# Tensor places in SBUF: weights of the last layer and of the down product in tensors of their own, attention, state and key tensors moved by 64-byte blocks

## The chip, the cores and the metric

The kernel runs on one core of one Trainium2 chip. The metric is the device time of one execution in microseconds (us), the median over several runs. The core has five engines that run side by side and wait for each other through semaphores: TensorE (PE; its weight loads are listed apart as PEld), VectorE (DVE), ScalarE (ACT), GpSimd (POOL) and SyncE (SP), which issues the transfers.

## What is computed

The input x has 16 sequences of 512 tokens with 256 features. Two branches start from the same layer norm, and both are added to x:

```python
xn = _layernorm(x, axis=-1)
x = x + attn(xn) + ffn(xn)
# attn: x @ up_w.T, a causal convolution of width 4, silu; q, k, g, tau projections;
#       gated linear attention in chunks, state 64 x 512; times silu(gate); rms norm; @ down_w.T
# ffn
h = jax.nn.silu(_tlin(x, w1_w, w1_s)) * _tlin(x, w2_w, w2_s)
h = jax.nn.gelu(_tlin(h, h1_w, h1_s), approximate=False)
h = jax.nn.gelu(_tlin(h, h2_w, h2_s), approximate=False)
return _tlin(h, w3_w, w3_s)
```

The ffn weights are ternary (-1, 0, 1), of sizes 256 to 1024 (w1, w2), 1024 to 1024 (h1, h2) and 1024 to 256 (w3).

## The kernel before, in words

**Tiling.** A sequence is worked off in two halves of 256 tokens, so there are 32 halves. A loop of 15 rounds (`rounds`) runs both halves of a sequence, and the last sequence stands behind it. All weights lie in SBUF from the start on. They come in 27 chunks of 128 x 1024 elements; each goes by DMA into a staging slot, from there ACT copies it into its place as fp32r, and DVE makes the low part (for `up`, `gate`, `proj`, `down`) or compares it with the original (for the ternary ones). Each activation is kept as a high and a low fp32r tensor, so that a product with ternary weights takes two matmuls, and one with the other weights three.

**Order of a half on TensorE.** z and up products, layer 1 (w1, w2) mixed with gate and input gate, transposes, the q/k/g/tau projection, layer h1, the small products of the attention, layer h2, in its middle `state_update` (first half of a sequence only, L604 to L607) and `outputs` (L613 to L628), transposes of the next layer norm (L453), layer w3 (32 matmuls of 256 columns), the down product (24 matmuls of 256 columns), and the sum for the rms norm (L679, two products, recorded as four). All of the wide products are issued by the helper `wide`, so they have one line, L383. The order is written out by hand in the program. There is no scheduler.

**Who is stationary and who moves.** `pe.matmul(out, a, b)` loads `a` into the array and streams `b` through it; a profile row prints `out<-b,a`: what moves comes first. In the hidden layers the weights (`wwhole`) are stationary and the activations (`xnth`, `xntl`, `hid0h`, `hid0l`, `hid1h`, `hid1l`) move. In w3 and in the down product it is the other way round: the activations are stationary (`hid0h`, `hid0l`; `parth`, `partl`) and the weights move (`wwhole`; `whi`, `wlo`). In `outputs`, `parth` and `partl` (then `vh`, `vl`, the values) are stationary and `atth`, `attl` move; in the second half of a sequence `stateh` and `statel` are stationary too, and `kdq` (then the queries) moves. In `state_update`, `kdq` (then the keys) is stationary and `parth`, `partl` move.

```python
for c in range(NC):                                                # w3, L383 through wide
    mm = wide(fb[2 * c][:, 0:H], [(a, wb) for a in parts(exact, hid0h[:, k, t], hid0l[:, k, t])], ...)
pairs += [(parth[:, k, t], wh), (partl[:, k, t], wh), (parth[:, k, t], wl)]   # down
first = [(vh[:, 0, cols], atth[:]), (vh[:, 0, cols], attl[:]), (vl[:, 0, cols], atth[:])]   # outputs
```

**Places.** Tensors are laid end to end in a partition, each start rounded up to 32 bytes. `lie_off(n)` puts in a gap so that the next tensor starts n blocks of 64 bytes behind the place of `wwhole`, modulo 512 bytes. In what follows a **place** is that number, 0 to 7 (`wwhole` is at 0 by definition). A step within a tensor (another weight block, another k) is a multiple of 512 bytes in all of the products named here, so that the place of an operand is that of its tensor.

**Probes that are in the program.** While the weights still come in, TensorE runs filler products without use for the result: `plain(bank, count, weights_at, moving_at)` issues `count` matmuls of 256 columns, stationary from `whi` shifted by `weights_at` elements of 4 bytes, moving from `wwhole` shifted by `moving_at` elements. 16 elements are one block of 64 bytes. `shifted` issues, for each pair in its list, two narrow products and then 14 of the full size. The lists, in the order of the program (L424 and L428):

```python
plain(3, 34)
shifted(0, [(0, 16), (0, 32)])
shifted(2, [(0, 48), (0, 64), (0, 80), (0, 96)])
shifted(2, [(0, 112), (0, 128), (0, 8), (8, 8), (16, 0), (32, 0), (64, 0), (80, 160), (24, 104), (16, 96)])
```

Of the kernel before, what the change touches and what calls it, by code (L numbers as in the profile page):

```python
# [6 lines left out]
F32 = mybir.dt.float32  # L7
F32R = mybir.dt.float32r
ALU = mybir.AluOpType
ACT = mybir.ActivationFunctionType  # L10

P = 128
# [25 lines left out]
COMB = CHUNKS.index("comb")  # L38
SPLIT = {"up": 0, "gate": 1, "proj": 2, "down": 3}


LOADS = [(n, m) for n in ("w1", "h1", "h2") for m in range(FB)] + [("w3", 0), ("w3", 1)]

WHOLE = {n: i for i, n in enumerate(c for c in CHUNKS if c not in SPLIT and c != "comb")}

# [34 lines left out]
def layer_program(nc, x, stage_w, ig1t, ig2t, convw, convb, projb, resw, normw, s1, s2, sh1, sh2, s3, ident,  # L80
                  masks, out):
    ctx = ExitStack()
    with ctx:
        def sb(name, shape, dt=F32):
            return ctx.enter_context(nc.sbuf_tensor(name, shape, dt))
# [23 lines left out]
        wwhole_place = next_place()  # L109
        wwhole = sb("wwhole", [P, len(WHOLE), STAGE], F32R)  # L110
        whi = sb("whi", [P, len(SPLIT), STAGE], F32R)
# [26 lines left out]

        xin = sb("xin", [P, HALVES, NC, H])
        lie_off(7)  # L140
        xnth, xntl = sb("xnth", [P, HB, N], F32R), sb("xntl", [P, HB, N], F32R)
# [32 lines left out]
        sqsum = work[:, DB * N + NC * H:]  # L174
        att = sb("att", [P, NC, CH])
        atth, attl = sb("atth", [P, 2, CH], F32R), sb("attl", [P, 2, CH], F32R)
        stateh, statel = sb("stateh", [P, DI], F32R), sb("statel", [P, DI], F32R)
        kdq = sb("kdq", [P, N], F32R)
        kd, qhl = kdq[:].rearrange("p (c a k) -> p c a k", c=NC, a=2), kdq[:]
# [73 lines left out]
        def stage_slot(n):  # L253

            return (sgate[:].rearrange("p d t -> p (d t)"), shift[:].rearrange("p d t -> p (d t)"),
                    v[:].rearrange("p c d -> p (c d)"), raw[:].rearrange("p a b t -> p (a b t)"), stage_more[:, 0, :], stage_more[:, 1, :],
                    mixed[:], small[:, 0:STAGE])[n % SLOTS]

        def rows(c):
# [119 lines left out]
        def _(pe):  # L379
# [14 lines left out]
            def ffn_weight(exact, name, k, m):  # L394


                if exact:
                    return (wwhole[:, WHOLE[f"w3{k // 4}"], (k % 4) * H:(k % 4 + 1) * H] if name == "w3" else
                            wwhole[:, WHOLE[f"{name}{k}"], m * P:(m + 1) * P])
                if name == "w3":  # L400
                    return stream[:, LOADS.index((name, k // 4)) % 2, (k % 4) * H:(k % 4 + 1) * H]
                if name == "w2":
                    name, k = "w1", HB + k
                return stream[:, LOADS.index((name, m)) % 2, k * P:(k + 1) * P]
# [13 lines left out]

            up, w10 = whi[:, SPLIT["up"], :], wwhole[:, WHOLE["w10"], :]

# [39 lines left out]
            def half(seq, p, last, exact):  # L460
# [207 lines left out]
                for c in range(NC):  # L668
                    t = slice(c * CH, (c + 1) * CH)
                    pairs = []  # L670
                    for k in range(DB):
                        wh, wl = split_w("down", k, 0, H, H)
                        pairs += [(parth[:, k, t], wh), (partl[:, k, t], wh), (parth[:, k, t], wl)]
                    mm = wide(ab[3][:, c * H:(c + 1) * H], pairs)
# [27 lines left out]
        def _(act):  # L702
# [7 lines left out]
            for n, name in enumerate(CHUNKS):  # L710
# [8 lines left out]
                if name == "down":  # L719
                    for d in range(DB):  # L720
                        mul = act.activation(whi[:, SPLIT[name], d * H:(d + 1) * H], stage_slot(n)[:, d * H:(d + 1) * H], ACT.Copy,
                                             scale=normw_s[:, d:d + 1])
                    mul.then_inc(prep_act, 1)
                elif name in SPLIT:
                    act.activation(whi[:, SPLIT[name], :], stage_slot(n), ACT.Copy).then_inc(prep_act, 1)
                else:
                    act.activation(wwhole[:, WHOLE[name], :], stage_slot(n), ACT.Copy).then_inc(prep_act, 1)  # L727

# [160 lines left out]
        def _(dve):  # L889
# [42 lines left out]
            for n, name in enumerate(CHUNKS):  # L932
# [30 lines left out]
                dve.wait_ge(prep_act, n + 1)  # L963
                if name in SPLIT:
                    if name == "down":
                        for d in range(DB):
                            t = slice(d * H, (d + 1) * H)
                            st = dve.scalar_tensor_tensor(wlo[:, SPLIT[name], t], stage_slot(n)[:, t], normw_s[:, d:d + 1],
                                                          whi[:, SPLIT[name], t].bitcast(F32), ALU.mult, ALU.subtract)
                        st.then_inc(prep_dve, 1)  # L970
                    else:
                        low(wlo[:, SPLIT[name], :], stage_slot(n), whi[:, SPLIT[name], :]).then_inc(prep_dve, 1)
                else:

                    if n > 1:
                        dve.wait_ge(prep_dve, n - 1)
                    dve.scalar_tensor_tensor(flags[:, n % 2, :], stage_slot(n), 1.0, wwhole[:, WHOLE[name], :].bitcast(F32), ALU.mult,
                                             ALU.not_equal, accum_out=inexact[:, WHOLE[name]:WHOLE[name] + 1]).then_inc(prep_dve, 1)
# [347 lines left out]
```

## Time and profile before

| what | value |
|---|---|
| median of 3 runs | 1945.26 us (1943.17 to 1946.41) |
| the profiled execution | 1944.75 us |
| span of its instructions | 1943.0 us |
| PE busy | 1926.5 us (99%) |
| PEld, weight loads | 1907.6 us (98%) |
| DVE / ACT / POOL busy | 1586.9 (82%) / 1296.4 (67%) / 81.2 us (4%) |
| granted TensorE clock | 0.998 |
| PE's share of the chain that ended last | 95% |

A matmul's record lasts longer than the time that it takes from its successor: they overlap. A 256-column matmul has a record of 276 to 283 ns, while the next one starts some 113 to 120 ns later. What counts for the time is this distance from start to start, called the **interval** below. Where a timeline row has n equal matmuls in one stretch without a gap, its second number is n - 1 intervals and one record.

### The profile page before, as it was taken

How to read it: one execution, taken by the hardware profiler on the slowest of the kernel's cores; microseconds unless marked ns; L12 is line 12 of the kernel's file. 1: busy time of each engine (PE TensorE's matmuls, PEld its weight loads, DVE VectorE, ACT ScalarE, POOL GpSimd, SP SyncE). 2: the span in 40 equal slices, each digit the busy share in tenths (PEclk: the TensorE clock that was granted, in tenths of full speed). 3: DMA queues.
4: the chain of work that ended last, by engine and by line, in shares of the span. 5: the costliest groups of instructions: out<-in, count | busy, mean ns of one | idle time of the engine just before them, and what ended most of it. 6: DMA issues, size and time to landing. Idle time of an engine off the chain costs nothing.

```text
span 1943.0 us, 46120 instructions
## 1 busy us (share of the span) xinstructions
PE 1926.5 (99%) x16804; PEld 1907.6 (98%) x16804; DVE 1586.9 (82%) x4304; ACT 1296.4 (67%) x2687; POOL 81.2 (4%) x136
## 2 busy tenths in 40 slices
PE   8999999999999999999999999999999999999998
PEld 7999999999999999999999999999999999999998
DVE  7788888888788887888888788787888878878887
ACT  5676667766676766666766677675667666667565
POOL 0000000000000000000000000000000000000000
PEclk9999999999999999999999999999999999999999
DMA  8000000000000000000000000000000000000000
GB/s 308 7 12 12 12 2 12 12 12 12 12 1 12 12 12 12 11 2 12 12 12 12 7 7 12 12 12 12 1 12 12 12 12 12 1 12 12 13 7 8
DMA packets 23538, 34.19 MB, mean 18 GB/s; under 512 B 3170, under 2 KB 19810, under 8 KB 23364
## 3 DMA queue, kind: packets, MB, share of 16 engines
q1 hardware_dynamic: 23364, 31.43, 4.8%
q8 instruction: 162, 2.65, 0.6%
q14 instruction: 12, 0.10, 0.0%
HBM read 23.04 MB, written 8.39 MB: 16 GB/s over the span
## 4 chain that ended last, share of the span: by engine, by line
PE 95%; issue 2%; ACT 1%; DVE 1%; SPq 1%; DMA 0%; POOLq 0%; POOL 0%; DVEq 0%; ACTq 0%
PE fb L383 65%; PE ab L383 21%; PE ab L593 2%; PE ab L628 1%; PE ab L529 1%; PE ab L518 1%; PE ab L453 1%; PE ab L583 1%; PE fb L679 1%; SPq L289 0%; PE ab L590 0%; PE ab L469 0%; ACT wwhole L727 0%; PE ab L606 0%; DMA shift<-stage_w 0%
## 5 line engine op out<-in xcount | busy, mean ns | idle before, releaser
L383 PE MATMUL fb<-hid1h,wwhole 128*128 128x256 f32 x2048 | 474.7, 279 | 0.0
L383 PE MATMUL fb<-hid1l,wwhole 128*128 128x256 f32 x2048 | 468.5, 276 | 0.0
L383 PE MATMUL fb<-hid0l,wwhole 128*128 128x256 f32 x2048 | 465.9, 276 | 0.0
L383 PE MATMUL fb<-hid0h,wwhole 128*128 128x256 f32 x2048 | 465.8, 276 | 0.0
L383 PEld LDWEIGHTS fb<-hid1h,wwhole 128*128 128x128 f32 x2048 | 384.6, 188 | 3.9 <-ACT raw L839 0.2
L383 PEld LDWEIGHTS fb<-hid1l,wwhole 128*128 128x128 f32 x2048 | 384.7, 188 | 0.0
L383 PEld LDWEIGHTS fb<-hid0h,wwhole 128*128 128x128 f32 x2048 | 384.4, 188 | 0.0
L383 PEld LDWEIGHTS fb<-hid0l,wwhole 128*128 128x128 f32 x2048 | 384.4, 188 | 0.0
L839 ACT ACTIVATE raw<-fb,sh_s 128x256 f32<-128x256 f32 x512 | 212.9, 466 | 143.2 <-PE fb L383 135.1
L383 PE MATMUL fb<-xntl,wwhole 128*128 128x256 f32 x1024 | 237.5, 276 | 0.0
L383 PE MATMUL fb<-xnth,wwhole 128*128 128x256 f32 x1024 | 237.5, 276 | 0.0
L1005 DVE SCALAR_TENSOR_TENSOR shift<-xbuf,convw_s,shift 128x256 f32<-128x256 f32 x384 | 168.9, 482 | 59.4 <-ACT shift L742 57.8
L896 DVE TENSOR_TENSOR hid0l<-raw,hid0h 128x512 fp32r<-128x512 f32 x256 | 175.8, 687 | 23.2 <-ACT hid0h L750 18.9
L383 PEld LDWEIGHTS fb<-xntl,wwhole 128*128 128x128 f32 x1024 | 192.3, 188 | 1.3
L383 PEld LDWEIGHTS fb<-xnth,wwhole 128*128 128x128 f32 x1024 | 192.3, 188 | 0.0
L750 ACT ACTIVATE hid0h<-raw 128x512 fp32r<-128x512 f32 x256 | 163.0, 637 | 19.3 <-DVE raw L991 13.1
L383 PE MATMUL ab<-xnth,whi 128*128 128x256 f32 x512 | 142.0, 277 | 0.0
L383 PE MATMUL ab<-xntl,whi 128*128 128x256 f32 x512 | 141.9, 277 | 0.0
L383 PE MATMUL ab<-xnth,wlo 128*128 128x256 f32 x512 | 141.7, 277 | 0.0
L896 DVE TENSOR_TENSOR hid1l<-raw,hid1h 128x512 fp32r<-128x512 f32 x128 | 88.0, 688 | 61.6 <-ACT hid1h L750 61.6
L991 DVE SCALAR_TENSOR_TENSOR raw<-fb,s_s,mixed 128x256 f32<-128x256 f32 x256 | 114.8, 480 | 28.1 <-ACT mixed L760 20.6
L739 ACT ACTIVATE xbuf<-ab 128x512 f32<-128x512 f32 x64 | 37.7, 588 | 139.4 <-PE ab L383 139.4
(234 smaller groups left out, 4527.3 us busy)
## 6 DMA issues: line engine op xcount, KB each, us to landing
xin<-x SPq DMA_DIRECT2D x32, 256.0 KB, 2.6
out<-xin SPq DMA_DIRECT2D x32, 256.0 KB, 2.2
stage_more<-stage_w SPq DMA_DIRECT2D x6, 512.0 KB, 7.3
sgate<-stage_w SPq DMA_DIRECT2D x4, 512.0 KB, 4.7
shift<-stage_w SPq DMA_DIRECT2D x4, 512.0 KB, 5.4
v<-stage_w SPq DMA_DIRECT2D x4, 512.0 KB, 5.6
raw<-stage_w SPq DMA_DIRECT2D x3, 512.0 KB, 6.1
mixed<-stage_w SPq DMA_DIRECT2D x3, 512.0 KB, 8.4
```

Of the source, the lines that this page charges most:

```text
L383: mm = pe.matmul(o, a, b, start=start and i == 0, stop=stop and i == len(pairs) - 1)
L453: mm = pe.transpose(ab[2][:, h * N + c * CH:h * N + (c + 1) * CH], xn[:, c, h * P:(h + 1) * P], ident_s[:])
L518: pe.matmul(ab[2 + c][:], zs[:, c * CH:(c + 1) * CH], ig2s[:], start=True, stop=True).then_inc(ig_mm.sem, 1)
L529: mm = pe.transpose(ab[c][:, d * P:(d + 1) * P], xbuf[:, d, W - 1 + c * CH:W - 1 + (c + 1) * CH], ident_s[:])
L583: pe.matmul(ab[3][:, 0:CH], kx, t1[rows(1), :], start=True, stop=True).then_inc(dg_mm.sem, 1)
L593: mm = pe.matmul(lev_out[i][:, c, :], lev_k[i][rows(c), :], lev_q[i][rows(c), :], start=True, stop=True)
L739: act.activation(xbuf[:, 2 * b:2 * b + 2, W - 1:], ab[b][:].rearrange("p (d t) -> p d t", d=2), ACT.Copy).then_inc(x_ev.sem, 1)
L750: act.activation(dst[:, 2 * b:2 * b + 2, :], src, ACT.Copy).then_inc(done.sem, 1)
L839: act.activation(raw[:, b % 2, j, :], fb[b][:, j * N:(j + 1) * N], ACT.Gelu, scale=scales[:, 2 * b + j:2 * b + j + 1]).then_inc(done.sem, 1)
L896: return dve.tensor_tensor(dst, src, hi.bitcast(F32), ALU.subtract)
L991: dve.scalar_tensor_tensor(raw[:, (m // 2) % 2, m % 2, :], fb[m % 4][:, N:2 * N], s2_s[:, m:m + 1], silu1[:, m % 4, :], ALU.mult, ALU.mult ...
L1005: dve.scalar_tensor_tensor(shift[:, d, :], xbuf[:, d, j:j + N], convw_s[:, d, j:j + 1], shift[:, d, :], ALU.mult, ALU.add).then_inc(conv_d ...
```

## The change

No instruction is added, removed or put elsewhere in its engine's order; the same transfers are issued from the same queue. Only addresses differ, and these are the places (in blocks of 64 bytes from `wwhole`, modulo 512 bytes):

| tensor | used as | place before | place after |
|---|---|---|---|
| w3 weights (`w30`, `w31`) | moving in w3, beside `hid0h`, `hid0l` at 7 | 0 (in `wwhole`) | 6 (`wlast`) |
| down weights | moving in down, beside `parth`, `partl` at 7 | 0 (in `whi`, `wlo`) | 6 (`dhi`, `dlo`) |
| `atth`, `attl` | moving in `outputs`, beside `parth`, `partl` at 7 | 3 | 6 |
| `kdq` | stationary in `state_update` beside `parth`, `partl` at 7; moving beside the state | 3 | 0 |
| `stateh`, `statel` | stationary in `outputs` | 3 | 1 |
| small tensors behind (`stats` ... `nb`) | scalars and statistics | 3 and on | 1 and on |
| `wwhole`, `whi`, `wlo` (rest), `xin`, `xnth` to `att` | | 0, 0, 0, 3, 7 ... 3 | the same |

`whi` and `wlo` get three chunks in place of four, `wwhole` 20 in place of 22, so that `whi` to `xin` lie up to 16384 bytes lower, at the same place modulo 512. From `xnth` to `att` the addresses are those of before.

```diff
-SPLIT = {"up": 0, "gate": 1, "proj": 2, "down": 3}
+SPLIT = {"up": 0, "gate": 1, "proj": 2}
-WHOLE = {n: i for i, n in enumerate(c for c in CHUNKS if c not in SPLIT and c != "comb")}
+WHOLE = {n: i for i, n in enumerate(c for c in CHUNKS if c not in SPLIT and c not in ("comb", "down"))}
+FIRST = len(WHOLE) - 2
-        wwhole = sb("wwhole", [P, len(WHOLE), STAGE], F32R)
+        wwhole = sb("wwhole", [P, FIRST, STAGE], F32R)
...
         xin = sb("xin", [P, HALVES, NC, H])
+        lie_off(6)
+        wlast = sb("wlast", [P, 2, STAGE], F32R)
+        dhi, dlo = sb("dhi", [P, STAGE], F32R), sb("dlo", [P, STAGE], F32R)
         lie_off(7)
         xnth, xntl = sb("xnth", [P, HB, N], F32R), sb("xntl", [P, HB, N], F32R)
...
         att = sb("att", [P, NC, CH])
+        lie_off(6)
         atth, attl = sb("atth", [P, 2, CH], F32R), sb("attl", [P, 2, CH], F32R)
+        lie_off(0)
+        kdq = sb("kdq", [P, N], F32R)
+        lie_off(1)
         stateh, statel = sb("stateh", [P, DI], F32R), sb("statel", [P, DI], F32R)
-        kdq = sb("kdq", [P, N], F32R)
...
+        def whole(name):
+            i = WHOLE[name]
+            return wwhole[:, i, :] if i < FIRST else wlast[:, i - FIRST, :]
...
-                        wh, wl = split_w("down", k, 0, H, H)
+                        wh, wl = (w[:, k * H:(k + 1) * H] for w in (dhi, dlo))
```

The places where `wwhole[:, WHOLE[name], :]` stood now call `whole(name)`, and ACT and DVE write `dhi` and `dlo` where they wrote the fourth chunk of `whi` and `wlo`.

## Rows read from the trace of the kernel before

**Rows 1.** The page: busy times, granted clock by slice, and the last chain.
```profile
PE 1926.5 (99%) x16804; PEld 1907.6 (98%) x16804; DVE 1586.9 (82%) x4304; ACT 1296.4 (67%) x2687; POOL 81.2 (4%) x136
...
PEclk9999999999999999999999999999999999999999
...
PE 95%; issue 2%; ACT 1%; DVE 1%; SPq 1%; DMA 0%; POOLq 0%; POOL 0%; DVEq 0%; ACTq 0%
```

**Rows 2.** Timeline of PE, first half: second w3 matmul, end of down (start us, us).
```profile
105.16 0.28 PE L383 MATMUL fb<-wwhole,hid0l 128*128 128x256 f32 x1
...
111.40 0.50 PE L679 MATMUL fb<-ones,work 128*128 128x1 f32 x4
```

**Rows 3.** The same two matmuls in the second half.
```profile
163.89 0.28 PE L383 MATMUL fb<-wwhole,hid0l 128*128 128x256 f32 x1
...
170.37 0.50 PE L679 MATMUL fb<-ones,work 128*128 128x1 f32 x4
```

**Rows 4.** The same two matmuls in the fifth half.
```profile
340.77 0.28 PE L383 MATMUL fb<-wwhole,hid0l 128*128 128x256 f32 x1
...
347.00 0.50 PE L679 MATMUL fb<-ones,work 128*128 128x1 f32 x4
```

**Rows 5.** Timeline of PE at the start: the probes (0,16), (0,64), (0,80).
```profile
12.69 1.75 PE L424 MATMUL fb<-wwhole,whi 128*128 128x256 f32 x14
...
24.05 1.83 PE L424 MATMUL fb<-wwhole,whi 128*128 128x256 f32 x14
...
25.94 1.75 PE L424 MATMUL fb<-wwhole,whi 128*128 128x256 f32 x14
```

**Rows 6.** The same view: the probes (0,112), (0,128).
```profile
30.59 1.76 PE L424 MATMUL fb<-wwhole,whi 128*128 128x256 f32 x14
...
32.43 1.84 PE L424 MATMUL fb<-wwhole,whi 128*128 128x256 f32 x14
```

**Rows 7.** The same view: the probes (16,0), (80,160), (24,104), (16,96).
```profile
38.12 1.81 PE L424 MATMUL fb<-wwhole,whi 128*128 128x256 f32 x14
...
43.79 1.81 PE L424 MATMUL fb<-wwhole,whi 128*128 128x256 f32 x14
...
45.67 1.81 PE L424 MATMUL fb<-wwhole,whi 128*128 128x256 f32 x14
...
47.55 1.81 PE L424 MATMUL fb<-wwhole,whi 128*128 128x256 f32 x14
```

**Rows 8.** Timeline of PE: `outputs`, one d of a second half.
```profile
157.34 0.28 PE L383 MATMUL ab<-attl,parth 128*128 128x256 f32 x1
157.46 0.29 PE L383 MATMUL ab<-atth,partl 128*128 128x256 f32 x1
157.59 0.28 PE L383 MATMUL ab<-kdq,stateh 128*128 128x256 f32 x1
157.70 0.28 PE L383 MATMUL ab<-kdq,statel 128*128 128x256 f32 x1
157.82 0.39 PE L628 MATMUL ab<-att,v 128*128 128x128 f32 x2
```

**Rows 9.** Timeline of PE: `state_update`, then the first product of `outputs`.
```profile
97.72 0.39 PE L604 MATMUL ab<-parth,kdq 128*128 128x512 f32 x1
97.95 0.63 PE L606 MATMUL ab<-partl,kdq 128*64 128x512 f32 x2
98.41 0.39 PE L607 MATMUL ab<-parth,kdq 128*128 128x512 f32 x1
98.64 0.28 PE L383 MATMUL ab<-atth,parth 128*128 128x256 f32 x1
```

**Rows 10.** Groups of PE by form: a hidden layer, w3, both in all halves.
```profile
L383 PE MATMUL fb<-hid0l,wwhole 128*128 128x256 f32 x2048 | 465.9, 276 | 0.0
...
L383 PE MATMUL fb<-wwhole,hid0h 128*128 128x256 f32 x512 | 123.4, 284 | 0.0
```

More of the change, by code:

```diff
@@ L397, in ffn_weight @@
                 if exact:
-                    return (wwhole[:, WHOLE[f"w3{k // 4}"], (k % 4) * H:(k % 4 + 1) * H] if name == "w3" else
-                            wwhole[:, WHOLE[f"{name}{k}"], m * P:(m + 1) * P])
+                    return (whole(f"w3{k // 4}")[:, (k % 4) * H:(k % 4 + 1) * H] if name == "w3" else
+                            whole(f"{name}{k}")[:, m * P:(m + 1) * P])
                 if name == "w3":
@@ L416, in parts @@
                 return aps if exact else tuple(a.bitcast(F32) for a in aps)
-            up, w10 = whi[:, SPLIT["up"], :], wwhole[:, WHOLE["w10"], :]
+            up, w10 = whi[:, SPLIT["up"], :], whole("w10")
             def plain(bank, count, weights_at=0, moving_at=0):
@@ L720, in _ @@
                     for d in range(DB):
-                        mul = act.activation(whi[:, SPLIT[name], d * H:(d + 1) * H], stage_slot(n)[:, d * H:(d + 1) * H], ACT.Copy,
+                        mul = act.activation(dhi[:, d * H:(d + 1) * H], stage_slot(n)[:, d * H:(d + 1) * H], ACT.Copy,
                                              scale=normw_s[:, d:d + 1])
@@ L726, in _ @@
                 else:
-                    act.activation(wwhole[:, WHOLE[name], :], stage_slot(n), ACT.Copy).then_inc(prep_act, 1)
+                    act.activation(whole(name), stage_slot(n), ACT.Copy).then_inc(prep_act, 1)
             def half(seq, p, last):
@@ L963, in _ @@
                 dve.wait_ge(prep_act, n + 1)
-                if name in SPLIT:
+                if name in SPLIT or name == "down":
                     if name == "down":
@@ L967, in _ @@
                             t = slice(d * H, (d + 1) * H)
-                            st = dve.scalar_tensor_tensor(wlo[:, SPLIT[name], t], stage_slot(n)[:, t], normw_s[:, d:d + 1],
-                                                          whi[:, SPLIT[name], t].bitcast(F32), ALU.mult, ALU.subtract)
+                            st = dve.scalar_tensor_tensor(dlo[:, t], stage_slot(n)[:, t], normw_s[:, d:d + 1],
+                                                          dhi[:, t].bitcast(F32), ALU.mult, ALU.subtract)
                         st.then_inc(prep_dve, 1)
@@ L976, in _ @@
                         dve.wait_ge(prep_dve, n - 1)
-                    dve.scalar_tensor_tensor(flags[:, n % 2, :], stage_slot(n), 1.0, wwhole[:, WHOLE[name], :].bitcast(F32), ALU.mult,
+                    dve.scalar_tensor_tensor(flags[:, n % 2, :], stage_slot(n), 1.0, whole(name).bitcast(F32), ALU.mult,
                                              ALU.not_equal, accum_out=inexact[:, WHOLE[name]:WHOLE[name] + 1]).then_inc(prep_dve, 1)
```

## Prediction

> **What bounds the kernel now.** I read the page first. TensorE is busy for 1926.5 of 1943.0 us, its weight loads for 1907.6 us, and 95% of the chain that ended last is TensorE's; the clock was granted in full in every slice [rows 1]. So a change of places can move the time only through the pace of the matmul stream. DVE (82%) and ACT (67%) have room, and their instructions keep their count, shape and order.
>
> Next I read the groups of PE by form. Records of a hidden layer last 276 ns on average, those of w3 with `hid0h` 284 ns [rows 10]: same shape, but operands at other places and in other roles. As records overlap, I then went to the timeline and read intervals, start to start. In the first half the 55 intervals from the second matmul of w3 to the end of the down product take 111.40 - 105.16 = 6.24 us, 113.5 ns each [rows 2]. In the second half the same 55, at the same addresses, take 170.37 - 163.89 = 6.48 us, 117.8 ns each [rows 3]. The fifth half takes 6.23 us again [rows 4]. I read this stretch in all 32 halves: 9 are like rows 2 (every fourth one from the first on, and the very last), 23 are like rows 3, and nothing lies between. One pair of places has **two stable paces**, and what was before on the engine selects one. The loss reaches the total: from rows 2 to rows 3 a half lasts 163.89 - 105.16 = 58.73 us, while the three halves from rows 3 to rows 4 take 176.88 us, 58.96 each.
>
> Last I read the probes. A row of 14 matmuls is 13 intervals and one record of 0.28 us. I write (s,m) for the places of the stationary and the moving operand in blocks.
> - (0,1) and (0,5): 1.75 us, 113.1 ns. (0,4): 1.83 us, 119.2 ns [rows 5].
> - (0,7): 1.76 us, 113.8 ns, its first intervals included. (0,8), which is (0,0): 1.84 us, 120.0 ns [rows 6].
> - (1,0), (5,2), (1.5,6.5), (1,6): 1.81 us each, 117.7 ns [rows 7].
>
> So the place matters, by up to 7 ns of 120. An even distance gives 119 to 120. An odd distance gives 113 where the stationary operand is at 0, and 117.7 in each of the four probes where it is not. The distance alone does not decide: (0,7) and (1,0) are both one block below, and they take 113.8 and 117.7 ns.
>
> On this point the Trainium skill speaks against the change: SBUF — State Buffer, section "SBUF: two separate sides", says that on the engine side only the port pair that VectorE and GpSimd share causes contention, and that TensorE never waits for anyone. By that rule no place could cost anything, the sum would be zero and the time 1945.3 us. Rows 5 and 6 disagree with it, 113.1 against 120.0 ns for one form of instruction at one clock, so I go by the rows.
>
> **The change, part by part.**
>
> *w3 and down, 56 matmuls in each of 32 halves.* The stationary operand stays at 7, the moving one goes from 0 to 6: from (7,0) to (7,6). No row shows (7,6). The nearest is (1,0): the same distance, the stationary operand also at an odd block, the moving one also at an even block; the other three of rows 7 are of the same kind and give the same 117.7 ns. The pair before, (7,0), is of this kind too, and runs at 117.8 ns in 23 halves. I take it that (7,6) behaves as (7,0) does, with about as many halves at the good pace: 0 us. Lower end, the pace of rows 2 in all halves: 23 x 0.24 = -5.5 us. Upper end, the 120.0 ns of rows 6 in all of them: 55 x 120.0 = 6.60 us a half, so 23 x 0.12 + 9 x 0.36 = +6.0 us.
>
> *`outputs`.* The four intervals before the fp32 product take 157.82 - 157.34 = 0.48 us, 120 ns each on average, one of them 0.13 [rows 8]; the seconds of the halves have 4 x 16 = 64 such groups. After the change each pair is one of (7,6), (1,6), (1,0), for which rows 7 give 117.7 ns: 4 x 2.3 ns x 64 = -0.6 us. The first halves have two such intervals per group and no state, 128 in all; I leave them as they are. Lower end, 113.1 ns everywhere: 256 x 6.9 ns = -1.8 us and 128 x 6.9 = -0.9 us, together -2.7. Upper end: rows 8 already stand at the worst average of any row, so 0. The wait after each fp32 product is not a matter of the moved places, and stays.
>
> *`state_update`, 16 times.* Its four products of 512 columns take 98.64 - 97.72 = 0.92 us [rows 9]. The keys go from 3 to 0 as stationary operand, the values stay at 7 as the moving one: (0,7), the pair of the hidden layers, which runs at its best. Four times 2 x 113.1 ns is 0.905 us, so 16 x 0.015 = -0.2 us. Upper end, 6.9 ns on each: 64 x 6.9 = +0.4 us.
>
> *Everything else.* `wwhole`, `whi`, `wlo` keep place 0 and `xnth` to `att` keep their addresses, so the hidden layers, up, gate and the projection keep their pairs (0,7). The tensors behind `statel` are scalars and statistics of DVE, ACT and POOL; those engines are not the bound [rows 1], and a few ns on a small operation stay under the matmuls of the layer that runs beside it. If that cover were gone, 32 x some ten operations x 5 ns would be 1.6 us. Weight copies into `wlast`, `dhi`, `dlo` are as many and as long as before. The probes are not moved: their rows should return unchanged.
>
> **The sum:** 0 - 0.6 - 0.2 = -0.8 us. The span goes from 1943.0 to 1942.2, the execution from 1944.75 to 1943.95; the median of before stands 0.5 us above its profiled execution, so **1944.5 us**. The bounds add to -8.4 and +6.4 us. A measurement here tells apart about 0.2%, 3.9 us.
>
> **Rivals.**
> 1. *One block below is good wherever the stationary operand lies.* (7,6) has the distance of (0,7), the pair of all hidden layers, and would fall into the good pace from any start, as (0,7) does in the probe [rows 6]. For it: (7,0) reaches 113.5 ns in 9 halves, so a stationary operand at 7 does not exclude that pace [rows 2, 4], and the 117.7 of a single short probe may be the second stable pace of a pair that has a better one. Against it: (1,0) is the same distance and stayed slow [rows 7], with the three other odd pairs. Price: -5.5 - 0.8, down to -8.4 if `outputs` follows: 1937 to 1939, say 1938.5 us.
> 2. *A half-way case*: the pair is still two-paced, and the entry after the transposes now selects otherwise. With no slow half among w3 and down it is rival 1; with no good one it is 9 x 0.24 = +2.2 us, 1946.7 us; with half of them good, 7 more than now, -1.7 - 0.8, 1942.8 us. All but the first stay within 0.2%, and I count them with the forecast.
> 3. *Slower: the moving operand at 6 runs at the pace of even distances.* If the weight load of the next matmul, which runs beside the moving stream, starts late enough to meet it one block on, the odd distance of (7,6) acts as an even one, and w3 and down lock at 120.0 ns in place of 117.8 or 113.5. Price +6.0 - 0.8 + 0.6, as `outputs` gains nothing: about 1951 us. It decides the sign when the 1760 intervals, now at 116.6 ns on average (23 x 6.48 + 9 x 6.24 us over 1760), exceed 118.8 ns. For it: four pairs of rows 5 to 7 differ by a block and change pace. Against: none of the four odd pairs of rows 7 was above 117.7.
> 4. *The change does not do what it says.* The sizes add up to places 6, 6, 0 and 1 as in the table, and the streams use the new tensors; I give this nothing.
>
> **How the numbers follow.** Forecast with rival 2: 0.66. Rival 1: 0.27, since a pair with two paces has gone both ways at (7,0), while the nearest probe speaks against it. Rival 3: 0.07. So faster 0.27, same 0.66, slower 0.07. The likeliest case alone spans 1942 to 1948. The range takes in rival 1, down to 1937.8 us, and the all-slow half-way case with the scatter of a median (1.5 us) on top, up to 1948.5 us; it leaves out rival 3 and the last bit of the lower bound.
>
> **What would show it.** In the changed kernel the 55 intervals from the second w3 matmul to L679 should read 6.48 us in most halves and 6.24 in some. 6.24 us in all 32 proves rival 1, 6.6 us rival 3. The probe rows must be those of rows 5 to 7. `outputs` should show four intervals of 0.12 us with no 0.13 among them; 0.45 us for the four would be the lower end there. `state_update` should lose 0.01 to 0.02 us. The prediction is wrong in kind if the hidden layers' 276 ns move [rows 10], for then a place matters that was not moved, or addresses matter beyond 512 bytes.

## The result

The changed kernel takes **1962.03 us** (median of 4 runs, 1958.70 to 1962.23) against 1945.34 us for the kernel before (4 runs, 1943.17 to 1946.41): a ratio of 1.0082, with a 95% interval of 1.0070 to 1.0094. It is 0.8% slower, 16.7 us. The prediction, 1944.5 us within 1937.8 to 1948.5, was wrong: it priced at nothing the hidden layers, of which no operand was moved, and they cost 15.5 us. The likeliest case missed by 17.5 us, and the chance that it gave to slower, 0.07, was too small.

The page of the changed kernel, against [rows 1]: PE is busy 12.6 us longer, DVE and ACT as before, the clock as high. This execution took 1958.7 us.

```profile
span 1956.9 us, 46120 instructions
PE 1939.1 (99%) x16804; PEld 1920.3 (98%) x16804; DVE 1587.7 (81%) x4304; ACT 1295.4 (66%) x2687; POOL 81.5 (4%) x136
...
PE 95%; issue 2%; ACT 1%; DVE 1%; SPq 1%; DMA 0%; POOLq 0%; POOL 0%; DVEq 0%; ACTq 0%
...
L395 PE MATMUL fb<-hid1h,wwhole 128*128 128x256 f32 x2048 | 482.9, 282 | 0.0
L395 PE MATMUL fb<-hid1l,wwhole 128*128 128x256 f32 x2048 | 476.9, 279 | 0.0
L395 PE MATMUL fb<-hid0l,wwhole 128*128 128x256 f32 x2048 | 472.1, 278 | 0.0
```

The line numbers are higher by 12; L395 is the L383 of before. The third row answers to the first of [rows 10]: 276 ns there, 278 here, in a hidden layer of which no operand was moved. The groups of h1 and h2 carry the loss. The w3 and down products, which the change is about, got a little better.

**Where in a half.** The timeline of PE (start, us), second half: the last 32 matmuls of h2, which stand behind `outputs`, begin at 159.60 in the kernel before and end 3.73 us later, in every half. For the first half, before, then changed: first matmul of this last part, first transpose behind it.

```profile
100.87 0.37 PE L383 MATMUL fb<-hid1h,wwhole 128*128 128x256 f32 x1
...
104.61 0.60 PE L453 MATMUL ab<-ident_s,work 128*128 128x128 f32 x4
```

```profile
101.03 0.36 PE L395 MATMUL fb<-hid1h,wwhole 128*128 128x256 f32 x1
...
104.88 0.60 PE L465 MATMUL ab<-ident_s,work 128*128 128x128 f32 x4
...
105.44 0.28 PE L395 MATMUL fb<-wlast,hid0l 128*128 128x256 f32 x1
...
111.68 0.50 PE L691 MATMUL fb<-ones,work 128*128 128x1 f32 x4
...
164.25 0.28 PE L395 MATMUL fb<-wlast,hid0l 128*128 128x256 f32 x1
...
170.73 0.50 PE L691 MATMUL fb<-ones,work 128*128 128x1 f32 x4
```

The last part of h2 takes 3.74 us before and 3.85 changed, with the same addresses. Its first interval is 0.20 or 0.21 us in both kernels; behind it the matmuls start 117.7 ns apart in place of 113.3. It is so in all 32 halves. w3 and down (the last four rows) take 6.24 us in the first half and 6.48 in the second, and so on alternately: 15 slow halves in place of 23.

Now h1 in the eighth and in the ninth half of the changed kernel: first of its 128 matmuls, and the product behind them.

```profile
483.17 0.28 PE L395 MATMUL fb<-hid0h,wwhole 128*128 128x256 f32 x1
...
497.68 0.27 PE L592 MATMUL ab<-ident_s,k_sq 128*128 128x128 f32 x1
...
542.30 0.28 PE L395 MATMUL fb<-hid0h,wwhole 128*128 128x256 f32 x1
...
557.38 0.27 PE L590 MATMUL ab<-ident_s,small 128*128 128x128 f32 x1
```

14.51 and 15.08 us, 113.4 and 117.8 ns each. From the ninth half on, the projection, h1 and the first 96 matmuls of h2 are slow together in 11 of the first halves (of a sequence), and never in a second one. In these 11 halves all 248 matmuls go together, and the pace is there from the fourth interval of the projection on.

**The sum**, by the counts and against the trace of before: 11 halves x 248 intervals x 4.3 ns = +11.7 us; last part of h2, 32 x 0.12 = +3.8; w3 and down, 8 halves fewer x 0.24 = -1.9; together +13.6 us of the 13.9 that the spans differ by (1956.9 - 1943.0). Added up from the starts in the two traces it reads: projection, h1 and first part of h2 +11.4 (before has one stretch that is slow, see below), last part of h2 +4.1, w3 and down -1.7, `outputs` -0.5, `state_update` +0.1, all else +0.5. The other three executions took some 3.4 us more than the profiled one, which is what three more such halves would cost (248 x 4.3 ns = 1.07 us each). They have no trace here, so this is an inference. It has a rival: the time up to the first projection, in which the weights still come in, differs by 3.3 us among the traces of the table below (65.98 us in e2, 69.31 us in e4).

### The profile page after: what moved, and what is told of

Read it like the earlier page. It is cut to its first block, busy times and chain, and to the rows that moved or that the text cites. A ratio compares the mean times of both kernels' runs of the same rounds, so it can differ in the third digit from the quotient of the medians.

```text
span 1956.9 us, 46120 instructions
## 1 busy us (share of the span) xinstructions
PE 1939.1 (99%) x16804; PEld 1920.3 (98%) x16804; DVE 1587.7 (81%) x4304; ACT 1295.4 (66%) x2687; POOL 81.5 (4%) x136
## 4 chain that ended last, share of the span: by engine, by line
PE 95%; issue 2%; ACT 1%; DVE 1%; SPq 1%; DMA 0%; POOLq 0%; POOL 0%; DVEq 0%; ACTq 0%
PE fb L395 65%; PE ab L395 21%; PE ab L605 2%; PE ab L640 1%; PE ab L541 1%; PE ab L530 1%; PE ab L465 1%; PE ab L595 1%; PE fb L691 1%; SPq L301 0%; PE ab L602 0%; PE ab L481 0%; PE ab L618 0%; ACT wwhole L739 0%; DMA sgate<-stage_w 0%
## 5 line engine op out<-in xcount | busy, mean ns | idle before, releaser
L395 PE MATMUL fb<-hid1h,wwhole 128*128 128x256 f32 x2048 | 482.9, 282 | 0.0
L395 PE MATMUL fb<-hid1l,wwhole 128*128 128x256 f32 x2048 | 476.9, 279 | 0.0
L395 PE MATMUL fb<-hid0l,wwhole 128*128 128x256 f32 x2048 | 472.1, 278 | 0.0
L395 PE MATMUL fb<-hid0h,wwhole 128*128 128x256 f32 x2048 | 472.0, 278 | 0.0
L395 PEld LDWEIGHTS fb<-hid1h,wwhole 128*128 128x128 f32 x2048 | 385.9, 188 | 3.9
L395 PEld LDWEIGHTS fb<-hid1l,wwhole 128*128 128x128 f32 x2048 | 386.1, 189 | 0.0
L395 PEld LDWEIGHTS fb<-hid0l,wwhole 128*128 128x128 f32 x2048 | 385.5, 188 | 0.0
L395 PEld LDWEIGHTS fb<-hid0h,wwhole 128*128 128x128 f32 x2048 | 385.4, 188 | 0.0
L395 PE MATMUL fb<-xntl,wwhole 128*128 128x256 f32 x1024 | 237.5, 276 | 0.0
L395 PE MATMUL fb<-xnth,wwhole 128*128 128x256 f32 x1024 | 237.5, 276 | 0.0
L395 PEld LDWEIGHTS fb<-xntl,wwhole 128*128 128x128 f32 x1024 | 192.3, 188 | 1.3
L395 PEld LDWEIGHTS fb<-xnth,wwhole 128*128 128x128 f32 x1024 | 192.3, 188 | 0.0
L395 PE MATMUL ab<-xnth,whi 128*128 128x256 f32 x512 | 142.2, 278 | 0.0
L395 PE MATMUL ab<-xntl,whi 128*128 128x256 f32 x512 | 142.1, 278 | 0.0
L395 PE MATMUL ab<-xnth,wlo 128*128 128x256 f32 x512 | 142.1, 278 | 0.0
```

The lines of the kernel that those rows point to most:

```text
L395: mm = pe.matmul(o, a, b, start=start and i == 0, stop=stop and i == len(pairs) - 1)
```

## The experiments

Two theories were set against each other at first. **Entry:** a pair of places at odd distance has two stable paces, 113.3 and 117.7 ns; the phase, that is the exact moment at which a run of matmuls is entered, picks one, and the run keeps it. So a moved tensor costs in the unmoved run behind it. **Address:** something beyond 512 bytes, or the split tensors, slows the hidden layers directly.

All runs but the two with other probes, which come further down, in one table; "slow" counts halves in the profiled execution, which need not be the median one: it took 1958.70 us in the changed kernel, 1950.42 in e3, 1948.13 in x2. The ratio is an estimate of its own and not the quotient of the two medians (e3 and x2 would give 1.0036 and 1.0032). The first column of counts is projection, h1 and the first part of h2, the second the last part of h2, the third w3 and down.

| run | median us | before, measured beside it | ratio (95%) | long run slow | last part slow | w3, down slow |
|---|---|---|---|---|---|---|
| before | 1945.34 | | | 0 | 0 | 23 |
| changed | 1962.03 | 1945.34 | 1.0082 (1.0070 to 1.0094) | 11 | 32 | 15 |
| e1_weights | 1949.17 | 1945.92 | 1.0018 (1.0009 to 1.0028) | 0 | 0 | 32 |
| e2_att | 1950.95 | 1945.92 | 1.0026 (1.0015 to 1.0036) | 4 | 16 | 31 |
| e3_state | 1952.93 | 1945.92 | 1.0047 (1.0031 to 1.0064) | 0 | 32 | 32 |
| e4_split_at_0 | 1945.84 | 1945.92 | 1.0001 (0.9992 to 1.0011) | 1 | 0 | 23 |
| g16_after_tail | 1947.36 | 1944.90 | 1.0013 (1.0004 to 1.0023) | 0 | 0 | 17 |
| f16_before_w3 | 1949.75 | 1944.90 | 1.0027 (1.0016 to 1.0038) | 1 | 0 | 31 |
| f32_before_w3 | 1949.91 | 1944.90 | 1.0028 (1.0019 to 1.0038) | 0 | 0 | 31 |
| w2_weights_at_2 | 1947.11 | 1944.87 | 1.0014 (1.0004 to 1.0024) | 0 | 0 | 32 |
| w4_weights_at_4 | 1945.05 | 1944.87 | 1.0000 (0.9990 to 1.0009) | 0 | 0 | 23 |
| g16_w2 | 1946.87 | 1944.87 | 1.0010 (1.0000 to 1.0020) | 0 | 0 | 17 |
| x3_second_halves | 1944.12 | 1945.23 | 0.9995 (0.9985 to 1.0004) | 0 | 16 | 1 |
| x1_before_transposes | 1956.39 | 1945.23 | 1.0058 (1.0040 to 1.0076) | 8 | 0 | 31 |
| x2_same_w6 | 1951.51 | 1945.23 | 1.0040 (1.0026 to 1.0053) | 5 | 0 | 1 |
| x4_64_columns | 1962.15 | 1945.23 | 1.0082 (1.0063 to 1.0100) | 13 | 0 | 30 |

In the kernel before, in g16_w2 and in x3_second_halves, one further half, the 31st each time, has only the first 96 matmuls of h2 slow. The other way round, the one slow half of e4 (the 23rd) and of f16 (the 7th) has only the projection and h1 slow: h1 takes 15.08 us there, and the first 96 matmuls of h2 take 11.00 again. So the pace can change between h1 and h2.

### One part of the change at a time

`e1_weights`: the changed kernel with the attention tensors where they were.

> Only the w3 and down weights at place 6 (wlast, dhi, dlo); attention, state and keys stay at 3 as before. Entry theory (each pair at odd distance has two stable paces, 113.3 and 117.7 ns; what streams just before a run of matmuls picks one, and the run keeps it): the last 32 matmuls of h2 behind outputs start from the phase of before and run at 113 to 114 ns in all halves, w3 and down are mixed; the time is 1937 to 1947 us. Address theory (the split tensors, or weights that lie 8 to 16 KB lower, slow the hidden layers whatever precedes them): hidden layers slow as in the changed kernel, 1955 to 1962 us. Against both: if w3 and down alone carried a cost, they would read over 118 ns.

`e2_att`: the kernel before, and in front of `atth, attl`

```diff
+        lie_off(6)
         atth, attl = sb("atth", [P, 2, CH], F32R), sb("attl", [P, 2, CH], F32R)
+        lie_off(3)
         stateh, statel = sb("stateh", [P, DI], F32R), sb("statel", [P, DI], F32R)
```

> Only atth and attl at place 6; weights, state and keys as before. Entry theory: outputs ends at another phase in the first halves (their last fp32r product moves atth), so the last 32 matmuls of h2 run at 117.7 ns in at least the 16 first halves, +2.3 us or more, and what follows shifts too; 1946 to 1960 us, with w3 and down at 117.7 or 113.5. Address theory: no change, within 2 us of before.

`e3_state`: the kernel before, with `kdq` at 0 and the states at 1, as in the change.

> Only kdq at 0 and stateh, statel at 1; weights and atth, attl as before. Entry theory: the first halves have no state in outputs and enter h2's last part as before, at 113; the second halves end outputs with kdq and statel at other places and enter at 117.7, +2.3 us from that part; 1944 to 1955 us. Address theory: no change, within 2 us of before.

`e4_split_at_0`: as e1, with `lie_off(0)` in front of `wlast`.

> The w3 and down weights in tensors of their own as in the changed kernel, but at place 0, and everything behind as before: all places modulo 512 bytes are those of before, only addresses beyond 512 bytes differ. Entry theory: the kernel before again, 1943 to 1947 us, w3 and down mixed 117.8 and 113.5, hidden layers at 113. Address theory: slower, 1950 us and up.

What follows. e4 is the kernel before again, in its time (ratio 1.0001) and in the count of 23 slow halves, though from the 25th half on they are not the same ones, behind the one slow h1. So the address theory falls: neither the split nor an address beyond 512 bytes costs anything that shows. Each of the other parts makes the kernel slower by itself, and each in its own way. With e1, w3 and down are slow in all 32 halves, so place 6 is no better for them. With e2 the unmoved last part of h2 is slow in exactly the 16 first halves, where `outputs` ends on `atth`. With e3 it is slow in all 32. I had expected only the second halves there: I had overlooked that `kdq`, too, stands in `state_update`, directly in front of `outputs` in the first halves. It is the only operand of TensorE in the first halves that e3 moves. In `e1` the stretch of the first half reads, second w3 matmul and end of down:

```profile
105.48 0.28 PE L392 MATMUL fb<-wlast,hid0l 128*128 128x256 f32 x1
...
111.97 0.50 PE L688 MATMUL fb<-ones,work 128*128 128x1 f32 x4
```

6.49 us, slow, at the addresses at which the changed kernel has 6.24 (105.44 to 111.68 above). What differs is the last part of h2 in front: fast here, slow there. This is no general rule: in the second halves of the changed kernel, and in all halves of e3, w3 and down are slow behind a slow last part of h2.

### Two paces at one address

The same probe, in the same place of the program, between operands that were not moved, is fast in [rows 6] and slow in the changed kernel. It is (0,112), that is (0,7):

```profile
30.64 1.81 PE L436 MATMUL fb<-wwhole,whi 128*128 128x256 f32 x14
```

1.76 us there, 1.81 here, which is 113.8 and 117.7 ns. To see how common this is, two kernels had the probes at the start replaced: 16 runs of 14 matmuls, each behind one fp32 product of 64, 68, 72 or 76 columns.

```diff
-                    narrow((bank + i) % 4, 2)
+                    pe.matmul(fb[bank][:, 0:cols], up[:, 0:P].bitcast(F32), w10[:, 0:cols].bitcast(F32), start=True, stop=True)
                     plain((bank + i) % 4, 14, weights_at, moving_at)
```

> The kernel before with other probes at the start: 16 runs of 14 matmuls, stationary at place 0, moving at 7, 1, 3, 5 (four runs each), and in front of each run one fp32 product of 64, 68, 72 or 76 columns, so that the four runs of a pair are entered at four phases. (The filler products behind the comb load are 20 longer, so that the clock is up.) Entry theory: a pair at odd distance settles at 113.3 ns in some of its four runs and at 117.7 in others, whichever of the four places; no run at 120. If only the distance -1 (moving at 7) has two paces, as the probe rows of the kernels before and after could be read, then 1, 3 and 5 read 113.3 four times each. If each pair has one pace and only the stationary place matters, all 16 read 113.3.

> The same with the stationary operand at place 7 and the moving one at 6, 0, 2, 4: the same four distances (-1, 1, 3, 5) with both operands at other blocks. Entry theory: again two paces, by the phase of entry, and the count of slow runs is like that of the first probe kernel. My reading in the prediction (an odd stationary place makes the pair slow, 117.7 ns): all 16 at 117.7, except for moving at 0, which is known to have both.

Timeline of the first: two runs of (0,7), two of (0,1), the third of (0,3). A row of 1.84 to 1.86 us settles at 113.3 ns behind such an entry, one of 1.89 or 1.90 us at 117.7.

```profile
14.62 1.85 PE L424 MATMUL fb<-wwhole,whi 128*128 128x256 f32 x14
...
26.41 1.85 PE L424 MATMUL fb<-wwhole,whi 128*128 128x256 f32 x14
28.23 1.90 PE L424 MATMUL fb<-wwhole,whi 128*128 128x256 f32 x14
30.11 1.90 PE L424 MATMUL fb<-wwhole,whi 128*128 128x256 f32 x14
...
39.92 1.85 PE L424 MATMUL fb<-wwhole,whi 128*128 128x256 f32 x14
```

And of the second: (7,6), (7,6), (7,0), (7,2).

```profile
13.82 1.84 PE L424 MATMUL fb<-wwhole,whi 128*128 128x256 f32 x14
15.64 1.85 PE L424 MATMUL fb<-wwhole,whi 128*128 128x256 f32 x14
...
36.14 1.90 PE L424 MATMUL fb<-wwhole,whi 128*128 128x256 f32 x14
38.02 1.86 PE L424 MATMUL fb<-wwhole,whi 128*128 128x256 f32 x14
```

With the stationary operand at 0: moving at 7 four fast; at 3 two fast and two slow; at 1 and at 5 four slow each. With it at 7: moving at 6 three fast, one slow (behind a longer pause); at 2 four fast; at 0 and 4 four slow each. (0,1) and (0,5) were fast in [rows 5], behind another entry. So my rule of the stationary place is wrong on both sides: (0,1) can be slow, and (7,6) and (7,2) can be fast. In these two kernels the distance from stationary to moving counts: -1 gives four and three fast of four (stationary at 0 and at 7), 3 gives two and four, 1 and 5 give none at either place.

The times of these two, 1954.25 and 1959.31 us in one run each, beside 1943.96, are no measure of the probes: most of the difference is a stall that the last section shows.

### No address moved: one small product in another place

`g16_after_tail`: the changed kernel and, in front of the last part of h2,

```diff
+                        if b == 3:
+                            pe.matmul(fb[3][0:R, 0:16], up[:, 0:R], hid1h[:, 0, 0:16], start=True, stop=True)
                         hidden("h2", b, hid1h, hid1l, h2_mm)
```

> The changed kernel with one small product more per half, 16 stationary and 16 moving columns, between outputs and the last 32 matmuls of h2 (bank fb3, overwritten by them): it moves nothing in memory, and shifts the phase at which those 32 start. Entry theory: these 32, at 117.7 ns in all 32 halves of the changed kernel, go back to 113 to 114 ns in most halves (-4.5 us at best, less about 1 us for 32 extra products), although no address changes. Any theory by addresses alone: they stay at 117.7, and the time rises by about 1 us.

14.7 us came back (1962.03 to 1947.36) by adding work. The last part of h2 is fast in every half; and the projection, h1 and the first part of h2 are at 113 ns everywhere too, which I had not expected. The products are dearer than I thought. The first row is the added one:

```profile
101.03 0.25 PE L653 MATMUL fb<-hid1h,whi 128*16 128x16 f32 x1
101.14 0.36 PE L395 MATMUL fb<-hid1h,wwhole 128*128 128x256 f32 x1
...
104.87 0.60 PE L465 MATMUL ab<-ident_s,work 128*128 128x128 f32 x4
```

From 101.03 to 104.87 is 3.84 us, 0.11 for the product and 3.73 for the 32 matmuls: it costs as much as it saves there, and the gain is in the long runs. The expectation had 0.03 us for such a product.

`f16_before_w3` and `f32_before_w3`: the kernel before, with such a product of 16 or 32 columns between the transposes and w3.

> The kernel before with one product of 16 x 16 columns more per half, between the fp32 transposes and w3 (bank fb0, overwritten). Entry theory: w3 and down, slow in 23 halves before, change their pace in many halves, all good at best: -5.5 us plus about 1 us for the products, 1941 us; all slow at worst, 1948.5 us. By addresses alone: +1 us, the pattern of every fourth half unchanged.

> The same with 32 moving columns in the added product, that is, another phase. Entry theory: another count of slow halves in w3 and down than with 16; between 1941 and 1949 us. By addresses alone: the same as with 16, within 1 us.

Both make w3 and down slow in 31 halves, where before had 23: the entry decides, but neither length finds the good phase, and the two give the same pattern, all halves but the last. That another length gives another count, as I had expected, is not borne out here; it is by x1 and x4 below, with 8 and 13 slow long runs.

`x1_before_transposes`, `x4_64_columns` (the kernel before) and `x2_same_w6` (e1) have the product in front of the transposes:

```diff
+                if not first:
+                    pe.matmul(ab[2][0:R, 0:16], up[:, 0:R], w10[:, 0:16], start=True, stop=True)
                 for h in range(HB):
```

> The kernel before with a product of 16 x 16 columns in front of the transposes of the next layer norm, no address changed. Entry theory: w3 and down, slow in 23 halves, show another pattern: 1940 us if all are good (-5.5 us and about 1 us for the products), 1948 if all are slow. If only the fp32 transposes themselves set the phase: pattern as before, 1946 us.

> The same product, with the w3 and down weights at 6 (there slow in all 32 halves). Entry theory: many halves good; 1940 to 1948 us. If the transposes alone set the phase: all 32 slow, 1949 us.

> As the first, with 64 moving columns in the small product, another phase again. Entry theory: a count of slow halves that differs from that with 16 columns, 1940 to 1949 us. If the length does not matter, the phase is reset by the presence of the product alone: the same pattern as with 16.

x4 is the clearest of all. It has every address of the kernel before and takes 1962.15 us, as much as the changed kernel. Its h1 in the ninth half:

```profile
544.96 0.28 PE L383 MATMUL fb<-hid0h,wwhole 128*128 128x256 f32 x1
...
560.04 0.27 PE L580 MATMUL ab<-ident_s,small 128*128 128x128 f32 x1
```

15.08 us again. Its sum is 13 x 1.07 + 7 x 0.24 = 15.6 us of its 18.4 us of span (1961.4 - 1943.0); of the 2.8 us left, 2.0 stand at the 31 added products, which lengthen the stretch of the transposes by 0.06 us each. x2 shows the other side: against before, w3 and down are good in 22 halves more, -5.3 us, and the projection, h1 and h2 turn slow in 5 halves, +5.3 us; the products cost 1.9 us again, of 3.3 us by which the spans differ. My expectation for x1, 1940 to 1948 us, left the projection out and missed by 8 us.

### Which end the first halves inherit

`x3_second_halves` is g16 with `if b == 3 and p == 1`.

> The changed kernel with the small product in front of h2's last part in second halves alone. Inheritance theory: first halves keep a slow last part of h2 (16 x 0.14 = 2.3 us) but no longer have slow projection, h1 and h2, as the end of the second half before them is changed; w3 and down are good in first halves, as in the changed kernel, and in second halves, as with the product in all halves. About 1942 us. If the first halves' long streams stay slow, the product in the first halves was what cured them: 1950 to 1958 us.

The pattern is as the inheritance theory of the expectation has it: the last part of h2 stays slow in the 16 first halves, and the projection and h1 are fast in all, though only the half in front of them got a product. In the ninth half:

```profile
540.19 0.28 PE L395 MATMUL fb<-hid0h,wwhole 128*128 128x256 f32 x1
...
554.70 0.27 PE L590 MATMUL ab<-ident_s,small 128*128 128x128 f32 x1
```

The time, 1944.12 us, is 2 us above what I expected, as 16 products cost 16 x 0.12 us, which I had left out. It is the best version found, 1.1 us under the kernel before as measured beside it, a ratio of 0.9995 with an interval from 0.9985 to 1.0004: not resolved from no change.

What hands the phase on is not shown, and the traces speak against a plain inheritance along TensorE's own stream. The seventh half of the changed kernel is fast and the ninth slow, yet the 185 intervals from w3 of the half in front up to the product before the projection agree within 2 ns. And there is a second engine in it. In the ninth half, then in the tenth, which is a second half and fast:

```profile
538.01 1.23 DVE L908 TENSOR_TENSOR partl<-shift,parth 128x1024 fp32r<-128x1024 f32 x1 [0.45 <-ACT parth L796]
...
539.31 0.19 PEld L395 LDWEIGHTS ab<-parth,whi 128*128 128x128 f32 x1
```

```profile
597.90 1.23 DVE L908 TENSOR_TENSOR partl<-shift,parth 128x1024 fp32r<-128x1024 f32 x1 [0.45 <-ACT parth L796]
...
599.12 0.48 PE L530 MATMUL ab<-ig2s,zs 98*128 98x512 f32 x1
599.20 0.19 PEld L395 LDWEIGHTS ab<-parth,whi 128*128 128x128 f32 x1
```

The projection waits for `partl`, which VectorE writes. In the tenth half it was ready at 599.13, and the first weight load follows its predecessor's product by 0.08 us. In the ninth it was ready at 539.24 only, and the load stands 0.15 us behind the product (539.16, shown in the last section) and 0.07 us behind VectorE. In the 16 traces of the table the load is held up like this in 229 of 512 halves, all of them first halves, and never the 31st. All 43 halves with a slow projection are among them; none of the 283 others is slow. The three cases of h2 alone are alike: its first matmul starts 0.26 to 0.30 us behind the small product in front, where 0.20 us is usual; two others as late, in e4 and g16, stayed fast. So every run that turned slow at the projection began with a late operand from another engine, and second halves, in which the load is never held up, stayed fast throughout. It is not enough by itself: in the changed kernel the third, fifth and seventh half are held up by as much, within 5 ns, and stay fast. No run moved VectorE's instruction, so this stands as a finding of the traces and not as a tested cause.

### The place of the w3 and down weights

> The w3 and down weights in tensors of their own at place 2, three blocks above their stationary operands at 7; all else as before. In the probes (7,2) settled at 113 in four of four entries behind an fp32 product, (7,0) in none. If those entries stand for the one behind the transposes, w3 and down run at 113 to 114 in nearly all halves: -5.5 us, 1939 to 1942 us. If only the body's own entry phase counts, any count of slow halves is possible, up to all 32: 1947.5 us.

> The same at place 4. In the probes (7,4) settled at 117.7 in four of four entries. If the probes stand for the body: w3 and down slow in all 32 halves, 1947 to 1948 us. Otherwise any count.

> The changed kernel with the small product in front of h2's last part, and the w3 and down weights at place 2 in place of 6. Here w3 and down are slow in 17 halves with place 6. By the probes they are good in all: 1947.4 - 17 x 0.24 = 1943.3 us; by entry alone, anything from 1943 to 1951 us, and the first halves may shift as well.

`w2` has all 32 halves slow, like e1 with place 6; `w4` has 23, and the same every-fourth-half pattern as place 0; g16_w2 has the 17 of g16. The probes did not stand for the body: by them 2 should have been good and 4 bad. But places four blocks apart are alike in the body: 6 as 2, 4 as 0. In the probes they are alike for the moving places 1 and 5, 0 and 4, nearly so for 6 and 2 (three and four fast), and not for 7 and 3 (four and two fast).

## Why the prediction was wrong

**What bounds the kernel** held: PE's pace alone, with DVE and ACT unchanged.

**The two paces** were read rightly, and then confined to (7,0). The prediction says "One pair of places has two stable paces, and what was before on the engine selects one." The second half of that sentence names the cause of nearly the whole result, if VectorE's late `partl` is counted with what was before. The first half is false: (0,7), (0,1), (0,3) and (7,6) have both as well.

**"Everything else: ... keep their pairs (0,7)"**, priced at nothing, is the step that failed. It measured +15.5 us (11.4 + 4.1 between the two traces, 11.7 + 3.8 by the counts). I took the good pace of the hidden layers as a property of their addresses. The trace of before held the counterexample. Its 31st half, below behind the 29th: first of the first 96 matmuls of h2, and the product behind them.

```profile
1735.94 0.38 PE L383 MATMUL fb<-hid1h,wwhole 128*128 128x256 f32 x1
...
1746.94 0.39 PE L604 MATMUL ab<-parth,kdq 128*128 128x512 f32 x1
```

```profile
1853.75 0.36 PE L383 MATMUL fb<-hid1h,wwhole 128*128 128x256 f32 x1
...
1865.14 0.39 PE L604 MATMUL ab<-parth,kdq 128*128 128x512 f32 x1
```

11.00 and 11.39 us, so one stretch of (0,7) in 32 was slow already, with a late entry of its own:

```profile
1853.72 0.19 PEld L383 LDWEIGHTS fb<-hid1h,wwhole 128*128 128x128 f32 x1 [0.19 <-ACT raw L839]
```

I had read w3 and down in all halves, and the hidden layers only by their mean.

**DVE and ACT "have room"** was true of their busy time. But in the first halves the moment at which VectorE hands over `partl` sets where the projection starts, and with it whether 248 matmuls can turn slow. The prediction has no term for that.

**w3 and down, 0 us** was near by luck: -1.7 us in the change, within the bounds. The reason given was wrong. The pace is not set by an odd stationary place. With the weights moved alone (e1) all 32 halves are slow, +2.2 us; in the changed kernel all first halves are fast, behind a last part of h2 that turned slow.

**`outputs` and `state_update`, -0.8 us**: the two traces read -0.5 us for `outputs`, where the prediction had -0.6, and +0.1 us for `state_update` (0.920 and 0.924 us each), where it had -0.2. Where they mattered was in what they hand on, which the prediction did not price.

**The rivals** were all about the pace of moved pairs. Rival 3 had the right sign by a wrong mechanism: w3 and down never reached 120 ns. Its chance counted the wrong thing. The mark set for it, "if the hidden layers' 276 ns move ... addresses matter beyond 512 bytes", pointed at the right row and named the wrong cause: e4 shows that they do not.

**The rule of the Trainium skill** (SBUF — State Buffer, section "SBUF: two separate sides"), that TensorE never waits for anyone there, gives 1945.3 us if one concludes from it that no place can cost anything. The measured 1962.03 us, from addresses alone, disagrees with that. No run here says where in the chip the 4.3 ns are lost.

## What to carry to other kernels

When one stretch of a trace shows two paces at the same addresses, look for both paces in every stream of the engine, half by half, before calling any of them safe: a mean of 276 ns hides a pace that has not yet been selected badly. A tightly packed matmul stream takes its pace from the way it is entered, by what ran before it and by the moment at which its first operand comes from another engine. So a change of places, order or length must be priced at the longest run behind it, here 248 matmuls of 4.3 ns in each sequence, not at the operands moved. A gain of half a per cent from such tuning is kept only as long as nothing in front changes: one 64-column product cost 0.8%.

## What the runs showed of the hardware

- **Pairs of places at an odd distance in blocks of 64 bytes have two stable intervals, 113.3 and 117.7 ns, for a 256-column fp32r matmul with its own weight load.** Both were seen for (0,1), (0,3), (0,5), (0,7), (7,0), (7,2), (7,4) and (7,6). The entry picks one, and it can last through 248 matmuls, across the small attention products between h1 and h2; in seven halves of the 18 traces it changed between h1 and h2. The difference at the entry is small: in the changed kernel the product in front of the projection stands 0.31 us before it in the seventh half and 0.32 us in the ninth, which is 1.07 us longer in all.

```profile
421.21 0.47 PE L530 MATMUL ab<-ig2s,zs 98*128 98x512 f32 x1
421.52 0.28 PE L395 MATMUL ab<-parth,whi 128*128 128x256 f32 x1
...
539.16 0.48 PE L530 MATMUL ab<-ig2s,zs 98*128 98x512 f32 x1
539.48 0.28 PE L395 MATMUL ab<-parth,whi 128*128 128x256 f32 x1
```

- **Places four blocks (256 bytes) apart act alike in the body** as far as tried: weights at 0 and 4 gave 23 slow halves each in the same pattern, at 2 and 6 all 32 each. The probes agree for (0,1) and (0,5), (7,0) and (7,4), but (0,3) had two slow runs of four where (0,7) had none, so the rule is not shown in general.
- **The scatter between executions may have the same source in part**; only one execution of each kernel has a trace, so this is an inference. Single executions of e2 range from 1947.01 to 1954.61 us, about seven halves of 1.07 us, while w4, with no slow long run in its trace, stays within 1942.97 to 1945.99. But e3 has none either and ranges from 1950.42 to 1955.98, and the time up to the first projection alone differs by 3.3 us between the traces of the table.
- **Two kernels stall at the loop's start.** In the two probe kernels, which have 20 more matmuls ahead of the loop, TensorE stands still near the 15th matmul of the first half in the rounds from the second on, 0.1 to 1.0 us, with no releaser in the profile ("issue"). The stretch from the end of down to the projection is 8.1 and 9.2 us longer over the whole program, of the 9.4 and 14.5 us by which the spans exceed that of before. In p2_probe_s7, the half at 648 us:

```profile
648.75 0.28 PE L383 MATMUL ab<-xntl,whi 128*128 128x256 f32 x1
649.25 0.38 PE L383 MATMUL ab<-xnth,wlo 128*128 128x256 f32 x1 [0.22 <-issue]
```

  No other kernel of the study has it. Why, was not tried.
- **Left open.** What physically makes 113.3 or 117.7 ns; why (7,2) settles at 113.3 ns in the probes and at 117.7 in the body; what decides, among the projections held up by VectorE, which turn slow; and whether an order exists in which the last part of h2, w3, down and the projection are all good without an added product. By the counts it would be worth about 5.5 us against the kernel before (23 x 0.24).
